# Gates' chain moved to ScalarE, idle TensorE products at three places, and one evacuation moved at the end of layer 1

## The chip, the cores and the metric

One core of one Trainium2 chip runs the whole program in one launch. The metric is the device time of an execution in microseconds (us), taken as the median of several runs. All tensors are fp32. TensorE runs at one of two granted clocks, 1.2 and 2.4 GHz, which the profile shows as 0.5 and 1.0.

## The reference

Two layers over x of 64 batches, 32 rows and 512 columns. Layer 0 is cross attention to a context of 257 rows, self attention and a linear layer with LoRA. Layer 1 begins with a gate over channels, then has self attention and a linear layer. The part around the change is the gate of layer 1:

```python
mu = jnp.mean(z, axis=(0, 2), keepdims=True)
var = jnp.mean((z - mu) ** 2, axis=(0, 2), keepdims=True)
zn = (z - mu) * jax.lax.rsqrt(var + EPS)
zn = zn * gamma.reshape(1, -1, 1) + beta.reshape(1, -1, 1)
return jax.nn.sigmoid(jax.nn.relu(zn))
...
A_S1 = _norm_active(_conv1d(crucial_x, conv_w), bn_gamma, bn_beta)
A_S2 = _norm_active(_conv1d(subcrucial_x, conv_w), bn_gamma, bn_beta)
return crucial_features * A_S1 + subcrucial_features * A_S2
```

The convolution has two input channels (maximum and mean over the channels chosen, or over the rest) and 7 taps along 512 positions. Its mean and variance go over all 64 batches and 512 positions. So no tile of layer 1 can begin before every tile of layer 0 has ended and the statistics are known.

## The kernel before

x is kept in SBUF as 16 tiles of 128 rows (4 batches of 32 rows each). A first phase computes the cross attention of layer 0 (to about 1470 us of the span). The rest is `phase_rest`: `layer0` (self attention and LoRA layer, to about 1810 us), `mix_gates` (the gate's convolution, statistics and sigmoid, once for all batches) and `layer1`. Each of the three is a block of its own, with an end that all engines reach before the next block begins.

`layer0` and `layer1` work in four lanes: tile t uses lane t % 4, with PSUM banks `low` and `high` of 512 columns each. `over_lanes` writes out the order of the stages by hand: each stage has a slot number (`SLOTS0`, `SLOTS1`), each tile of the first eight and of the last four a start number (`STARTS0`, `STARTS1`), and every engine issues its stages in the order of start plus slot. The first stages are unrolled, the middle is a loop over four tiles that runs twice, and the last are unrolled again. An engine works through its queue strictly in that order. A stage waits for a semaphore against t + 1.

The stages that the change touches, with their lines:

- `tile_stats` (L926 to L935), on VectorE: bn_stats, bn_aggr and the addition of EPS, each waiting for the one before through semaphores "stats" and "aggr" of `norm_sems`.
- The end of `layer0` on TensorE: the last stage is `turn3` (four transposes, L961). On VectorE the last stage is `reduce_part` (L1344), of the two halves of the last tile.
- `mix_gates`: TensorE's convolution of 20 products of 128x128 by 128x128 (L1399) into one bank of PSUM, and two sums over partitions by a product with a matrix of ones (L1403, L1405). VectorE masks w_ffn (L1428), then copies the convolution to SBUF (L1431), sums (L1433), forms the mean (L1435), subtracts it (L1437), squares (L1441), sums (L1443), forms the variance (L1445), multiplies by the inverse root (L1447), applies gamma and beta (L1450) and relu (L1452). GpSimd takes the root (L1411, two instructions), ScalarE the sigmoid of 512 columns (L1417), VectorE writes `blend` (L1454, L1455).
- `layer1` on TensorE: `turn_mix` (L1537), `turn1` (L961), `qkv` (L1544 and L1547), `scores` (L1555), `values` (L1564), `project` (L1571), `turn2` (L961), `ffn` (L1577). On ScalarE: `xnT1` (L1591), `evac_qk` (L1598), `exps` (L1603), `spread_p` (L1611), `evac_ot` (L1617), `xnT2` (L1591). On VectorE among others `gate`, `add_rest`, `mix` (L1628, L1635, L1641), `add_mix` (L1645), `turn_probs` (L1682 to L1690), `add_proj` (L1695), `add_ffn` (L1699).

By the order numbers, TensorE's first stages in layer 1 are turn_mix of tiles 0 and 1, turn1 of tile 0, qkv of tile 0. Its last are values and project of tile 14, values of tile 15, turn2 of tile 14, project of tile 15, ffn of tile 14, turn2 and ffn of tile 15. ScalarE issues exps of tile 15 (41.722) ahead of evac_ot of tile 14 (41.749).

## Time and profile before

| | us |
|---|---|
| median of 3 runs | 2084.58 |
| the three runs | 2083.96, 2084.58, 2088.28 |
| the profiled execution's own time | 2082.45 |
| its span, first to last instruction | 2080.6 |
| mean granted clock over the span | 0.989 |

Start times in the rows are us from the start of the span. The first number of a timeline row is the start, the second the duration; "x8" counts instructions. One fp32 product on TensorE is two records, so a product of 128 columns is x2. In brackets stands how long the engine had been idle and what ended that. A row of the chain of waits has start, duration and the work.

### The profile page before, as it was taken

Reading aid. Unit: us, or ns where it says so; the run is one execution under the profiler, and the core shown is the slowest. Engines: PE = TensorE matmul, PEld = TensorE weight load, DVE = VectorE, ACT = ScalarE, POOL = GpSimd, SP = SyncE. Lnnn points to the kernel's source line nnn. Section 1 sums busy time; section 2 is a strip of 40 time slices with the busy share of each in tenths; the row PEclk is TensorE's granted clock in tenths of the full one; section 3 lists DMA queues with packets and bytes.
Section 4 is the critical chain, followed back from the end, with each engine's and each line's share of the span. In section 5 each row is a group of like instructions: output and inputs, shape, how many; then the busy total and the mean of one; then the engine's idle time right before and its main releaser. Section 6 shows DMA issues by size and latency. Waiting matters only on the chain. (4 is left out here: it accounts for less than half of the span.)

```text
span 2080.6 us, 36577 instructions
## 1 busy us (share of the span) xinstructions
PE 2011.5 (97%) x11304; PEld 1563.5 (75%) x11304; DVE 1296.1 (62%) x4403; ACT 740.4 (36%) x2037; POOL 677.5 (33%) x1068
## 2 busy tenths in 40 slices
PE   9999999999999999999999999999899999779997
PEld 7878778887887878788787878887566666455664
DVE  4745648475574836548474564847477676667775
ACT  3434434343343434334343433433232323122332
POOL 3333324233232422324242332423332333133332
PEclk9999999999999999999999999999999999889999
DMA  7100101010010101001010010111100000000000
GB/s 286 43 25 25 30 14 39 16 30 24 24 30 24 30 15 32 21 24 30 24 30 24 24 30 14 30 47 41 46 1 1 1 0 30 1 1 21 21 15 26
DMA packets 52572, 62.19 MB, mean 30 GB/s; under 512 B 14258, under 2 KB 48242, under 8 KB 51619
## 3 DMA queue, kind: packets, MB, share of 16 engines
q1 hardware_dynamic: 52514, 61.46, 9.4%
q8 instruction: 32, 0.52, 0.1%
q14 instruction: 26, 0.21, 0.0%
HBM read 54.00 MB, written 4.29 MB: 28 GB/s over the span
## 5 line engine op out<-in xcount | busy, mean ns | idle before, releaser
L438 PE MATMUL psLane<-hid,WkT 128*128 128x289 f32 x1536 | 402.4, 407 | 0.0
L438 PEld LDWEIGHTS psLane<-hid,WkT 128*128 128x128 f32 x1536 | 283.4, 190 | 72.3
L656 ACT ACTIVATE probs<-psLane,nmax 128x289 f32<-128x289 f32 x256 | 126.0, 497 | 430.1 <-DVE nmax L765 430.1
L622 ACT ACTIVATE KT<-psLane 96x289 f32<-96x289 f32 (+2 forms) x384 | 155.5, 405 | 149.9 <-PE psLane L438 147.7
L360 POOL TENSOR_TENSOR w_o<-w_o 128x192 f32<-128x192 f32 x64 | 39.0, 610 | 455.2 <-ACT w_o L631 455.2
L805 DVE MAX8 top<-work 128x8 f32<-128x257 f32 x512 | 180.3, 414 | 2.7
L320 POOL TENSOR_TENSOR tails<-probs,unit 128x66 f32<-128x66 f32 x128 | 38.2, 299 | 436.8 <-ACT probs L656 406.0
L428 PE MATMUL psLane<-xnT,WqT 128*128 128x128 f32 x1536 | 176.6, 275 | 0.0
L428 PEld LDWEIGHTS psLane<-xnT,WqT 128*128 128x128 f32 x1536 | 174.7, 192 | 0.3 <-issue 0.3
L525 PE MATMUL psLane<-WoT,OT 128*128 128x512 f32 x384 | 169.0, 597 | 1.4 <-DVE OT L785 1.4
L790 DVE TENSOR_TENSOR X<-X,psLane 128x512 f32 (+1 forms) x16 | 11.0, 688 | 253.9 <-PE psLane L525 253.9
L631 ACT ACTIVATE w_o<-psLane 128x384 f32<-128x384 f32 (+1 forms) x256 | 113.5, 451 | 153.4 <-PE psLane L451 153.4
L471 PE MATMUL psLane<-KT,QT 96*128 96x289 f32 x512 | 146.1, 406 | 1.3 <-ACT QT L645 1.3
L525 PEld LDWEIGHTS psLane<-WoT,OT 128*128 128x128 f32 x384 | 73.1, 192 | 86.7 <-issue 85.0
L762 DVE TENSOR_REDUCE rmax<-psLane 128x2 f32<-128x578 f32 x128 | 97.1, 758 | 64.2 <-PE psLane L471 62.8
L779 DVE TENSOR_TENSOR O<-psLane,rinv 128x384 f32<-128x384 f32 x64 | 35.7, 558 | 158.2 <-PE psLane L498 143.6
L940 POOL TENSOR_TENSOR lane_rstd<-lane_veps,neghalf 128x1 f32<-128x1 f32 x79 | 53.0, 671 | 188.8 <-DVE lane_veps L935 188.8
L471 PEld LDWEIGHTS psLane<-KT,QT 96*128 96x128 f32 x512 | 90.8, 190 | 22.7 <-issue 7.2
L494 PEld LDWEIGHTS psLane<-V,probsT 128*128 128x128 f32 x512 | 84.4, 190 | 30.0 <-issue 11.9
L451 PE MATMUL psLane<-WvT,hid 128*128 128x192 f32 x512 | 104.2, 326 | 0.0
L451 PE MATMUL psLane<-w_ffn 128*128 128x192 f32 x512 | 104.1, 326 | 0.0
L809 DVE MATCH_REPLACE8 work<-top,hid 128x257 f32<-128x257 f32 x256 | 102.2, 411 | 0.0
(213 smaller groups left out, 4126.7 us busy)
## 6 DMA issues: line engine op xcount, KB each, us to landing
hid<-in_ctxT SPq DMA_DIRECT2D x64, 514.0 KB, 3.8
y<-X SPq DMA_DIRECT2D x16, 256.0 KB, 2.0
X<-in_x SPq DMA_DIRECT2D x1, 3584.0 KB, 20.9
WqT<-in_WqT SPq DMA_DIRECT2D x4, 768.0 KB, 9.1
Vtail<-Vlat SPq DMA_DIRECT2D x128, 24.0 KB
WoT<-in_WoT SPq DMA_DIRECT2D x1, 3072.0 KB, 11.6
w_qkv<-in_w_qkv SPq DMA_DIRECT2D x2, 1536.0 KB, 6.3
w_ffn<-in_w_ffn SPq DMA_DIRECT2D x2, 1024.0 KB, 7.0
```

What stands on the lines that cost most here:

```text
L428: mm = pe.matmul(out[:, P * r:P * r + P], WqT[:, c, w:w + P], xnT[:, c, :], start=(c == 0), stop=(c == DC - 1))
L438: mm = pe.matmul(out[:, 0:S], WkT[:, c, P * k:P * k + P], hid[:, j, c, :], start=(c == 0), stop=(c == DC - 1))
L451: mm = pe.matmul(out, left(c), right(c), start=(c == 0), stop=(c == 1))
L471: mm = pe.matmul(psS[:, g % 2, 0:S], QT[:, g, j, :], KT[:, j % 2, g, :], start=True, stop=True)
L494: pe.matmul(out, probsT[:, g % 2, 0, :], V[:, j % 2, 0, cols], start=(g % 2 == 0), stop=False)
L525: mm = pe.matmul(psM, OT[:, n // G, n % G].rearrange("p j q -> p (j q)"), WoT[:, n, :], start=(n == 0), stop=(n == NKT * G - 1))
L622: ins = act.activation(KT[at:at + hi - lo, j % 2, g, :], psKV[lo:hi, kv_bank(t, 7 * j + k), 0:S], ACT.Copy)
L631: act.activation(vproducts[:, 2 * f:2 * f + n, :].rearrange("p a n -> p (a n)"), psKV[:, kv_bank(t, 7 * j + 3 + f), 0:VH * n], ACT.Copy).t ...
L656: act.activation(probs[:, g, :], psS[:, g % 2, 0:S], ACT.Exp, bias=nmax[:, g:g + 1], scale=XSCALE, accum_out=rsum[:, j % 2, g:g + 1]).then ...
L762: dve.tensor_reduce(rmax[:, 2 * h:2 * h + 2], psS[:, :, 0:S], AX.X, ALU.max).then_inc(rmax_done, 1)
L805: ins = dve.max(top[step // 2][:, c, :], src[:, c, :] if step == 1 else work[:, c, :])
L809: ins = dve.match_replace(work[:, c, :], picked[:, c, :], src[:, c, :] if step == 2 else work[:, c, :], GONE)
```

## The change

`mix_gates` is written anew. The convolution goes into four banks, one for each 128 output positions, and signals after each; VectorE masks w_ffn in four parts and sums each bank straight from PSUM (four instructions in the place of the copy and the sum). TensorE adds the four parts up by four products with `ones`, which now holds -1/(64*512), so that the mean comes out with its sign turned. ScalarE forms the squares with their sum (Square with an accumulator, one instruction for each of the two channels w), and after the root applies scale, offset and relu in one instruction for each w, then the sigmoid for each w, the first straight into `blend`. VectorE forms scale and offset on two columns. GpSimd takes the root of both columns in one instruction. Each ScalarE part opens with an activation on a column of scratch, Sigmoid in `mix_gates`, Exp in `layer1`.

`keep_busy` issues products of `ones` with `ones` whose output nobody reads: 10 at the end of `layer0`, 6 and 12 in `mix_gates`, 8, 10 and 4 ahead of the first turn_mix, turn1 and qkv of `layer1`, 2 ahead of project of tile 14 and 7 ahead of values of tile 15. On ScalarE, evac_ot of tile 14 gets the order number 41.65 and so goes ahead of exps of tile 15 (behind spread_p of tile 14). The two semaphores of `tile_stats` become one that counts by two.

```diff
-    dve.wait_ge(n["stats"], t + 1)
+    dve.wait_ge(n["stats"], 2 * t + 1)
     dve.memset(gate[:], 0.0)
-    dve.bn_aggr(small["mv"][:, u], small["stats"][:, u]).then_inc(n["aggr"], 1)
-    dve.wait_ge(n["aggr"], t + 1)
+    dve.bn_aggr(small["mv"][:, u], small["stats"][:, u]).then_inc(n["stats"], 1)
+    dve.wait_ge(n["stats"], 2 * t + 2)
...
+CLOSING1 = {("evac_ot", NT - 2): 41.65}
...
+            pe.wait_ge(ones_done, 1 + 2 * TB)
+            keep_busy(pe, ps[:, LANES - 1], ones, 10)
...
+def keep_busy(pe, out, ones, n):
+
+    for _ in range(n):
+        pe.matmul(out[:, 0:P], ones[:], ones[:], start=True, stop=True)
...
-            mm.then_inc(conv_done, 1)
-            pe.wait_ge(step, 2)
-            pe.matmul(sums, ones[:], part[:], start=True, stop=True).then_inc(sums_done, 1)
-            pe.wait_ge(step, 6)
-            pe.matmul(sums2, ones[:], part[:], start=True, stop=True).then_inc(sums_done, 1)
+                mm.then_inc(conv_done, 1)
+            pe.wait_ge(part_done, DC)
+            for o in range(DC):
+                mm = pe.matmul(sums, ones[:], part[:, o], start=(o == 0), stop=(o == DC - 1))
+            mm.then_inc(sums_done, 1)
+            keep_busy(pe, idle, ones, 6)
+            pe.wait_ge(squares_done, 2)
+            pe.matmul(sums2, ones[:], squares[:], start=True, stop=True).then_inc(sums_done, 1)
+            keep_busy(pe, idle, ones, 12)
...
+            pool.wait_ge(moment_ready, 1)
+            pool.tensor_tensor(rstd[:], moment[:], neghalf[:].to_broadcast([P, 2]), ALU.pow).then_inc(pow_done, 1)
...
+            act.activation(scratch[:, 0:1], neghalf[:], ACT.Sigmoid).then_inc(scratch_done, 1)
+            act.wait_ge(mean_ready, 1)
+            for w in range(2):
+                act.activation(sq[:, :, w], by_which[:, w], ACT.Square, bias=minus_mean[:, w:w + 1],
+                               accum_out=squares[:, w:w + 1]).then_inc(squares_done, 1)
+            act.wait_ge(scale_done, 1)
+            act.wait_ge(offset_step, 2)
+            for k, w in enumerate((1, 0)):
+                act.activation(Z[:, :, w], by_which[:, w], ACT.Relu, bias=offset[:, w:w + 1], scale=scale[:, w:w + 1])\
+                    .then_inc(relu_done, 1)
+                act.wait_ge(relu_done, k + 1)
+                act.activation(blend[:, :, 0] if w else Z[:, :, 0], Z[:, :, w], ACT.Sigmoid).then_inc(sig_done, 1)
...
+            for o in range(DC):
+                dve.tensor_tensor(late["w_ffn"][:, o], late["w_ffn"][:, o], late["ffn_mask"][:, o], ALU.mult)
+                dve.wait_ge(conv_done, o + 1)
+                dve.tensor_reduce(part[:, o], conv[:, o].rearrange("p (w b) -> p w b", w=2),
+                                  AX.X, ALU.add).then_inc(part_done, 1)
             dve.wait_ge(sums_done, 1)
+            dve.tensor_scalar(minus_mean[:], sums, 1.0, None, ALU.mult).then_inc(mean_ready, 1)
             dve.wait_ge(sums_done, 2)
+            dve.tensor_scalar(moment[:], sums2, -1.0, EPS, ALU.mult, ALU.add).then_inc(moment_ready, 1)
             dve.wait_ge(pow_done, 1)
+            dve.tensor_scalar(scale[:], rstd[:], affine[:, 0:1], None, ALU.mult).then_inc(scale_done, 1)
+            dve.wait_ge(scale_done, 1)
+            dve.tensor_tensor(offset[:], minus_mean[:], scale[:], ALU.mult).then_inc(offset_step, 1)
+            dve.wait_ge(offset_step, 1)
+            dve.tensor_scalar(offset[:], offset[:], affine[:, 1:2], None, ALU.add).then_inc(offset_step, 1)
+            dve.wait_ge(sig_done, 2)
+            dve.tensor_tensor(blend[:, :, 1, :], Z[:, :, 0, :], blend[:, :, 0, :], ALU.subtract)
...
+            def busy_until_first(t, n):
+
+                if isinstance(t, int) and t == 0:
+                    keep_busy(pe, high(LANES - 1), ones, n)
...
+            def busy_at_end(t, n):
+
+                if isinstance(t, int) and t >= NT - 2:
+                    keep_busy(pe, high(0), ones, n[t - NT + 2])
...
+            act.activation(scratch[:], neghalf[:], ACT.Exp).then_inc(s["table_loaded"], 1)
```

## Rows read from the trace of the kernel before

**Rows 1.** Page, busy time of each engine over the span
```profile
PE 2011.5 (97%) x11304; PEld 1563.5 (75%) x11304; DVE 1296.1 (62%) x4403; ACT 740.4 (36%) x2037; POOL 677.5 (33%) x1068
```

**Rows 2.** Stretches of 5 us: PE, PEld, DVE, ACT, POOL busy, clock, DMA share, GB/s
```profile
1800.00:1805.00 5.00, 1.00 (x6) 0.71 (x4) 4.44 (x10) 0.60 (x1) 2.16 (x2) 0.68 0.00 0
...
1810.00:1815.00 5.00, 4.42 (x20) 4.42 (x21) 2.69 (x3) 1.28 (x1) 0.00 (x0) 0.50 0.01 3
1815.00:1820.00 5.00, 2.98 (x24) 2.71 (x22) 1.81 (x4) 0.00 (x0) 0.00 (x0) 0.96 0.00 0
1820.00:1825.00 5.00, 0.38 (x2) 0.30 (x2) 3.21 (x7) 0.00 (x0) 1.07 (x2) 0.72 0.00 0
```

**Rows 3.** Timeline, end of layer 0 and the convolution
```profile
1804.14 1.11 PE L961 MATMUL psLane<-ident,lane_xn 128*128 128x128 f32 x4 [4.00 <-DVE lane_xn L945]
...
1807.09 2.62 DVE L1344 TENSOR_REDUCE Y<-lanes 128x16 f32<-128x512 f32 x4
...
1810.59 7.02 PE L1399 MATMUL psLane<-Y,band 128*128 128x128 f32 x40 [5.33 <-DVE Y L1425]
```

**Rows 4.** Timeline, the gates' chain
```profile
1819.11 0.38 PE L1403 MATMUL psLane<-part,ones 128*128 128x2 f32 x2 [1.50 <-DVE part L1433]
1819.53 0.16 DVE L1435 TENSOR_SCALAR moment<-psLane 128x2 f32<-128x2 f32 x1 [0.48 <-PE psLane L1403]
...
1822.57 1.07 POOL L1411 TENSOR_TENSOR mix_rstd<-moment,neghalf 128x1 f32<-128x1 f32 x2 [14.18 <-DVE moment L1445]
...
1826.32 0.42 DVE L1455 TENSOR_TENSOR blend<-Z 128x256 f32<-128x256 f32 x1
```

**Rows 5.** Chain of waits: 16 products of 128 columns at clock 1.00
```profile
1891.00 3.57 PE psLane L1544 x32
```

**Rows 6.** Timeline, ScalarE: activation with accumulator, and groups by shape
```profile
701.68 0.49 ACT L656 ACTIVATE probs<-psLane,nmax 128x289 f32<-128x289 f32 x1
702.06 0.20 ACT L656 ACTIVATION_READ_ACCUMULATOR probs<-psLane,nmax 128x1 f32 x1
```

**Rows 7.** Groups of instructions on ScalarE, shapes apart; last number before the bar: mean ns
```profile
L1598 ACT ACTIVATE lane_QK<-psLane,b_qk 128x128 f32<-128x128 f32 x64 | 18.0, 363 | 16.6 <-PE psLane L1547 16.6
L1603 ACT ACTIVATE lane_p<-lane_p 128x256 f32<-128x256 f32 x16 | 6.7, 418 | 23.6 <-POOL lane_p L1523 23.6
L1617 ACT ACTIVATE lane_xnT<-psLane 128x256 f32<-128x256 f32 x16 | 6.1, 382 | 28.2 <-PE psLane L1564 28.2
```

**Rows 8.** Timeline, opening of layer 1 on TensorE and ScalarE
```profile
1831.77 1.11 PE L1537 MATMUL psLane<-ident,lanes 128*128 128x128 f32 x4 [1.41 <-DVE lanes L1641]
...
1834.00 1.11 PE L961 MATMUL psLane<-ident,lane_xn 128*128 128x128 f32 x4 [1.12 <-DVE lane_xn L945]
...
1835.15 0.60 ACT L1591 ACTIVATE lane_xnT<-psLane 128x512 f32<-128x512 f32 x1 [9.07 <-PE psLane L961]
...
1835.80 5.50 PE L1544 MATMUL psLane<-lane_xnT,w_qkv 128*128 128x128 f32 x32 [0.69 <-ACT lane_xnT L1591]
```

**Rows 9.** Timeline, ScalarE's table load for Exp
```profile
1851.83 1.28 ACT L1603 ACT_TABLE_LOAD   x1
```

**Rows 10.** Timeline, TensorE after transposes in layer 1
```profile
1880.19 3.54 PE L1571 MATMUL psLane<-w_o,lane_xnT 128*128 128x512 f32 x4
```

**Rows 11.** Timeline, end of layer 1
```profile
2059.93 0.64 PE L1564 MATMUL psLane<-lanes,lane_V 128*32 128x128 f32 x16 [1.11 <-ACT lanes L1611]
...
2061.29 0.37 ACT L1617 ACTIVATE lane_xnT<-psLane 128x256 f32<-128x256 f32 x1
...
2061.70 1.98 PE L1571 MATMUL psLane<-w_o,lane_xnT 128*128 128x512 f32 x4 [1.13 <-ACT lane_xnT L1617]
...
2063.73 0.69 DVE L1695 TENSOR_TENSOR X<-X,psLane 128x512 f32<-128x512 f32 x1 [0.72 <-PE psLane L1571]
...
2064.80 0.64 PE L1564 MATMUL psLane<-lanes,lane_V 128*32 128x128 f32 x16 [1.11 <-ACT lanes L1611]
```

**Rows 12.** Register instructions of VectorE's sequencer at L931; ns min/median/max
```profile
L931 DVEq ALU_OP  x8: 40/40/47, 1603.7 to 1748.6; - x8
```

96 lines of the change are left out of this document (40 added, 56 removed).

## The prediction

> **What bounds the kernel now.** I read the page first. TensorE is busy 97% of the span [rows 1], so time can be won only where TensorE waits or runs slowly, and the granted clock of 0.989 says that slow stretches are short. Views by stretch then show where they are. Between layer 0 and layer 1 TensorE is busy 1.00 us of five, then 4.42 and 2.98 for the convolution, then 0.38 of five. The clock falls in the first of these stretches (0.68), is at 1.2 GHz through 1810 to 1815, is back at 2.4 GHz for most of the next (0.96) and falls again in the last (0.72) [rows 2]. Before each fall TensorE had done almost nothing for some us; before the rise it had worked without a pause from 1810.59 [rows 3].
>
> The timeline of that stretch shows one chain. VectorE's last reduction ends at 1807.09 + 2.62 = 1809.71, the convolution runs from 1810.59 to 1817.61 [rows 3], and then VectorE, TensorE, GpSimd and ScalarE hand one small result on to the next until blend is written at 1826.32 + 0.42 = 1826.74 [rows 4]. That is 9.13 us from the end of the convolution to blend, in which no tile can move. Then layer 1 opens, still at the low clock: four transposes take 1.11 us and the first 16 products of qkv 5.50 [rows 8], where the same work at the full clock takes 3.57 [rows 5]. The end of the kernel is a second chain: project of tile 14 waits for an evacuation on ScalarE [rows 11].
>
> **The change, part by part.** The sum is made against the profiled execution, whose own time is 2082.45 (span 2080.6). It lies 2.13 us under the median of the three runs, 2084.58. One idle product is two records. At the full clock 32 records take 3.57, so one product is 0.223; at the low clock 20 records took 4.42 in the stretch from 1810 [rows 2, 5], so one is 0.44.
>
> **(a) Ten products at the end of layer 0: 0.0.** TensorE's last transposes end at 1805.25 [rows 3]. Ten products take 2.2 at the full clock and 4.4 at the low one, to 1809.65 at the latest. VectorE's reduction, ending at 1809.71, hides them; without that cover they would cost up to 4.4. The semaphore for `ones` was raised early in the layer.
>
> **(b) The convolution: -2.3.** At 2.4 GHz throughout its 40 records take 40/32 x 3.57 = 4.46, in the place of 7.02 [rows 3, 5]: -2.56. If the ten products leave the clock where it was, the gain is 0; the low bound on a worse case is all 20 products at 0.44, which is 8.8, +1.8. Before, the clock rose 4.8 us into this work (0.96 over 1815 to 1820 leaves 0.4 us at the low clock [rows 2]); now TensorE begins that work 5.3 us earlier, with a pause of about 1 us. I take almost the whole gain, because the rise before came within the convolution itself, and leave 0.26 for a late rise. VectorE's four masks of 128x512 and four small reductions fit beside it; only the last reduction stays behind.
>
> **(c) The gates' chain: -1.9.** From the end of the convolution, in us:
> - last reduction of 128 columns, no such row; between the 0.16 of a two-column VectorE instruction and the 0.42 of one of 256 [rows 4]: 0.3, with the mask ahead of it some 0.1 late, so 0.4.
> - four products for the sum in the place of one: the one took 0.38, six more records at 3.57/32 = 0.11 make it 1.05 [rows 4, 5], done at 1.5.
> - mean with its sign turned: 0.2 with its wait [rows 4], at 1.7.
> - two squares with accumulators. The nearest pair, 289 columns, starts 0.38 apart within one instruction and its reading of the accumulator, which takes 0.20 more [rows 6]. That is about 0.5 each, 1.0 for the pair of 256: 2.8. Six idle products end at 1.5 + 1.34 = 2.9, 0.1 after; this overrun is a wait that was not there.
> - second sum 0.4, variance 0.2: at 3.5.
> - GpSimd: two roots took 1.07 [rows 4], one instruction for both takes 0.55 to 0.6: 4.1.
> - scale and offset: three VectorE instructions at 0.16 [rows 4] with waits: 4.7.
> - relu, sigmoid, relu, sigmoid, each of 256 columns. A copy of 256 takes 0.38 and an exponential of 256 0.42; a bias operand makes 128 columns take 0.36, and two operands were never used together [rows 7]. I take 0.6 for a relu and 0.42 for a sigmoid: 2.05 with waits, at 6.75. Bounds: 1.6 with no cost for operands, 2.6 if each instruction waits for the last to drain.
> - the final difference, 0.42 [rows 4]: 7.2.
>
> 9.13 - 7.2 = 1.9; the bounds of its terms give 1.0 to 2.5. The 12 products behind the second sum run from 3.3 to 6.0, beside the chain. At the low clock they would reach 8.6 and hold the end of the block by 1.4. Masking w_ffn in parts, and the load of ScalarE's table in front of the scratch sigmoid, lie beside the convolution as before.
>
> **(d) The opening of layer 1: -0.5, between -1.6 and +1.6.** In the clock times of before: turn_mix of tile 1 is ready at 1831.77 by VectorE, and ends at 1832.4 with transposes of 0.60. Eight products ahead of turn_mix of tile 0 take 1.8, hidden, since VectorE needs 2.2 for its three instructions. The ten products then run to 1834.6, while turn1 was ready at 1834.00 [rows 8]: 0.6 late, which the faster transposes about make up (1835.2 against 1835.11). The four products run to 1836.1 against 1835.80, 0.3 late. Then qkv takes 3.57 rather than 5.50 [rows 5, 8]: -1.9 + 0.3 = -1.6. The other end: the clock has fallen before the ten. Between the eight and the ten products TensorE has only transposes for 3.5 us. In layer 1 there is a row for it: after waits and transposes, project took 3.54, where it takes 1.98 elsewhere [rows 10, 11]. Then the ten take 4.4 from 1832.9 to 1837.3, turn1 ends at 1838.4, four products at 1839.3 (full clock by then), and qkv starts 3.5 late but runs at full clock: +1.6. A fall with a rise halfway through the ten gives about -0.1. I take -0.5, between this and the full gain. TensorE goes from qkv straight to the next stages, so what is won there is passed on.
>
> **(e) Exp's table in front: 0.0.** The load of 1.28 [rows 9] moves to ScalarE's idle time at the start of the layer. Its reader is VectorE, which has other tiles' stages in that queue, so I take 0; at most -1.3.
>
> **(f) The end: -0.7.** values of tile 14 end at 2059.93 + 0.64 = 2060.57, and evac_ot, which waited behind exps of tile 15, ran at 2061.29. Going ahead it can start at 2060.6 and end at 2061.0, with project at 2061.02 rather than 2061.70 [rows 11]: -0.68. exps of tile 15 is queued behind it and starts at 2061.0, 0.04 late, which VectorE's sum behind it absorbs. Two products (0.45) fit before project. add_proj of tile 14 follows project directly, and so do the norm, turn2, project of 15 and both ffn, so all of it shifts. Seven products (1.56) run from 2063.0 to 2064.6; values of tile 15 start at 2064.80 as before [rows 11].
>
> **(g) One semaphore for two: +0.1.** Its value is 2t + 1 and 2t + 2, which loops have to work out in registers; such an instruction takes 0.04 [rows 12]. Outside the loops values are constants. Only layer 1's loop (16 norms) could feel it: 0 to +1.3 at two for each norm.
>
> **The sum:** -2.3 - 1.9 - 0.5 - 0.7 + 0.1 = -5.3, so 2077.2 for a profiled execution like this one. Against the median it would be 2079.3. Part of those 2.13 us may be clock falls that hit other executions at the opening and the end, where TensorE has gaps, and which idle products would fill. I take off 0.7: **2078.6**.
>
> **Rivals.** A measurement tells about 0.2%, 4.2 us, from no change; faster begins at 2080.4.
>
> *The idle products are late themselves* (0.12). The opening is at its other end: -5.3 + 0.5 + 1.6 = -3.2, which is 2081.4. For it: a row of transposes is followed by a slow product. Against it: uninterrupted work raised the clock before.
>
> *The clock before is not won back by the ten products* (0.09). The convolution stays at about 7.0 and the opening gains nothing: -1.9 - 0.7 + 0.1 = -2.5, which is 2082.1. For it: the pause of 1 us in front of the convolution. Against it: the same shape raised it before.
>
> *A table switch inside the chain* (0.08). If Square is not in the table that Sigmoid uses, the second load lands between square and sigmoid, 1.28 once or twice [rows 9] on the path: -4.0 to -2.7 against -5.3, so 2079.9 to 2081.2. In this trace copies and Identity come between Exps with no further load; Square was never used. The Trainium skill (ScalarE: Activation LUTs, "Table sets: the hidden batching unit") says that cheap functions, relu, copy, identity and abs, are in every set, and does not name Square there; its budget of 2.7 us for a switch would make this case 2081.3 to 2084.0, while the row here has 1.28.
>
> *Idle products never hold the clock* (0.05), the slower side. They multiply constants; if they do not count as work, they only stand in the queue at 0.44 each. The place is the opening: eight end 1.3 after turn_mix is ready, which shifts VectorE behind it, ten run to 11.4 us after the layer's start, turn1 ends at 12.5, four at 14.3, and qkv starts 5.5 later than the 8.8 of before. In the gates six end 2.1 later than squares do and the twelve hold the block's end 1.6 beyond before. With -0.7 at the end that is +6.4: 2091. It decides from the point where the ten products start with the clock at 1.2 GHz and end so too.
>
> **How the numbers follow.** The forecast has 0.66, with a range of its own of 2075.5 to 2081, nearly all of it faster. Faster: 0.66 and half of the table's 0.08, 0.70. Same: the late products 0.12, the clock not won 0.09, half the table's, 0.25. Slower: 0.05. The range leaves out what is slower than "not won back" and the sum of all best bounds (-2.56 - 2.5 - 1.6 - 0.7, 2077.2 in median terms, less the 2.13 if all of it was falls: 2075.1): 2075 to 2082.5.
>
> **What would show it.** Right: TensorE's clock at 1.0 in 1810 to 1822; the convolution under 5 us; from its end to the last write of blend 6.7 to 8.1; no table load between Square and Sigmoid; at the opening, first 16 products of qkv about 3.6; evac_ot of tile 14 under 0.1 us after values, project 0.45 after. Wrong: an idle product still running when turn1's xn is ready by more than 1 us; the convolution near 7; ScalarE's six instructions of the chain summing over 3.7; a wait of values of tile 15 on products ahead of it.

## The result and the profile after

The changed kernel takes 2074.75 us, the median of five executions (2074.12 to 2076.66), beside 2084.58 for the kernel before in five executions of the same session (2083.81 to 2088.28). The ratio is 0.9951, with a 95% interval of 0.9939 to 0.9962: it is faster, by 9.8 us. The forecast was 2078.6 with a range from 2075.0, so the direction was right and the time lies 0.25 us below the range. The profiled execution took 2076.66 (span 2074.5, mean clock 0.995), where the one before took 2082.45 (2080.6, 0.989). Between these two the difference is 5.8 us, against a sum of 5.3. So most of what the forecast missed lies outside its sum by parts: in what it took the medians to be beside the two profiled executions. The experiments look for that, and for the one part of the sum that came out otherwise.

The busy times of the page of after, against [rows 1]:

```profile
PE 2021.7 (97%) x11428; PEld 1575.4 (76%) x11428; DVE 1291.7 (62%) x4404; ACT 743.1 (36%) x2046; POOL 676.0 (33%) x1067
```

TensorE has 124 more records, two each for the 59 idle products and the three more of the first sum. It is 10.2 us longer busy in a span 6.1 us shorter. A busy share can't tell the two kernels apart here (97% in both): the added work gives nothing to the output and stands where TensorE would have waited.

The stretches of [rows 2] come out like this (PE, PEld, DVE, ACT, POOL busy, clock, DMA share, GB/s):

```profile
1805.00:1810.00 5.00, 4.70 (x24) 4.51 (x22) 4.89 (x9) 0.60 (x1) 1.27 (x1) 0.58 0.00 0
1810.00:1815.00 5.00, 3.89 (x34) 3.89 (x35) 3.12 (x9) 1.49 (x2) 0.00 (x0) 1.00 0.01 3
1815.00:1820.00 5.00, 4.62 (x40) 4.37 (x39) 1.51 (x6) 1.02 (x4) 0.70 (x1) 1.00 0.00 0
1820.00:1825.00 5.00, 3.32 (x30) 3.16 (x30) 2.52 (x7) 3.33 (x6) 0.00 (x0) 1.00 0.00 0
1825.00:1830.00 5.00, 2.96 (x25) 2.53 (x24) 4.23 (x11) 0.00 (x0) 0.55 (x1) 1.00 0.00 2
1830.00:1835.00 5.00, 5.00 (x47) 5.00 (x46) 4.40 (x12) 0.60 (x1) 0.93 (x1) 1.00 0.01 3
...
1875.00:1880.00 5.00, 5.00 (x12) 2.46 (x11) 2.46 (x6) 1.98 (x5) 0.00 (x0) 0.75 0.14 52
```

The clock is at its lower level while the ten products at layer 0's end run (0.58 of the stretch), and at 2.4 GHz from the first product of the convolution on, through the gates and the opening. In [rows 2] the stretches from 1810 and 1820 stand at 0.50 and 0.72. It falls once more near 1875, with project of tile 0 under it.

The timeline of after, at the end of layer 0 and through the gates, answers to [rows 3, 4]:

```profile
1804.66 1.11 PE L961 MATMUL psLane<-ident,lane_xn 128*128 128x128 f32 x4 [4.00 <-DVE lane_xn L945]
1805.57 4.13 PE L1374 MATMUL psLane<-ones 128*128 128x128 f32 x20
...
1807.61 2.63 DVE L1348 TENSOR_REDUCE Y<-lanes 128x16 f32<-128x512 f32 x4
...
1811.11 4.73 PE L1416 MATMUL psLane<-Y,band 128*128 128x128 f32 x40 [1.42 <-DVE Y L1453]
...
1815.88 0.29 DVE L1459 TENSOR_REDUCE part<-psLane 128x2 f32<-128x128 f32 x1
...
1816.23 1.05 PE L1421 MATMUL psLane<-part,ones 128*128 128x2 f32 x8 [0.39 <-DVE part L1459]
...
1817.14 1.58 PE L1374 MATMUL psLane<-ones 128*128 128x128 f32 x12
...
1817.32 0.16 DVE L1462 TENSOR_SCALAR minus_mean<-psLane 128x2 f32<-128x2 f32 x1 [1.15 <-PE psLane L1421]
1817.52 0.47 ACT L1438 ACTIVATE sq<-psLane,minus_mean 128x256 f32<-128x256 f32 x1 [5.50 <-DVE minus_mean L1462]
...
1818.59 0.38 PE L1425 MATMUL psLane<-squares,ones 128*128 128x2 f32 x2
...
1819.25 0.70 POOL L1431 TENSOR_TENSOR mix_rstd<-moment,neghalf 128x2 f32<-128x2 f32 x1 [10.32 <-DVE moment L1464]
...
1820.77 0.56 ACT L1443 ACTIVATE Z<-psLane,mix_offset,mix_scale 128x256 f32<-128x256 f32 x1 [2.23 <-DVE mix_offset L1470]
...
1821.36 0.42 ACT L1446 ACTIVATE blend<-Z 128x256 f32<-128x256 f32 x1
1821.68 0.55 ACT L1443 ACTIVATE Z<-psLane,mix_offset,mix_scale 128x256 f32<-128x256 f32 x1
...
1822.71 0.43 DVE L1472 TENSOR_TENSOR blend<-Z,blend 128x256 f32<-128x256 f32 x1 [2.04 <-ACT Z L1446]
```

The ten products end at 1809.70, 0.5 before VectorE's last reduction (1810.24), and TensorE then waits 1.42 us. The convolution takes 4.73 where it took 7.02. From its end (1815.84) to blend (1823.14) are 7.30 us where there were 9.13. No table load stands between the square and the sigmoid.

The opening of layer 1, against [rows 8]:

```profile
1825.64 0.66 PE L1561 MATMUL psLane<-ident,lanes 128*128 128x128 f32 x4 [0.18 <-DVE lanes L1678]
...
1828.17 0.66 PE L1561 MATMUL psLane<-ident,lanes 128*128 128x128 f32 x4 [1.87 <-DVE lanes L1678]
1828.66 2.40 PE L1374 MATMUL psLane<-ones 128*128 128x128 f32 x20
1829.80 0.55 DVE L945 TENSOR_SCALAR lane_xn<-X,lane_mv,lane_rstd 128x512 f32<-128x512 f32 x1 [0.66 <-POOL lane_rstd L940]
1830.89 0.60 PE L961 MATMUL psLane<-ident,lane_xn 128*128 128x128 f32 x4
1831.33 1.06 PE L1374 MATMUL psLane<-ones 128*128 128x128 f32 x8
1832.22 3.79 PE L1573 MATMUL psLane<-lane_xnT,w_qkv 128*128 128x128 f32 x32
```

The transposes take 0.66 and 0.60 where they took 1.11, and the first 16 products of qkv 3.79 where they took 5.50. xn of tile 0 is ready at 1830.35 and the ten products end at 1831.06, so they do stand in its way, by about half a microsecond: what they cost is paid, and it is less than they give.

The end of layer 1, against [rows 11]:

```profile
2054.45 0.64 PE L1599 MATMUL psLane<-lanes,lane_V 128*32 128x128 f32 x16 [1.10 <-ACT lanes L1647]
2055.02 0.71 PE L1374 MATMUL psLane<-ones 128*128 128x128 f32 x4
2055.16 0.38 ACT L1653 ACTIVATE lane_xnT<-psLane 128x256 f32<-128x256 f32 x1 [0.76 <-PE psLane L1599]
2055.59 1.99 PE L1607 MATMUL psLane<-w_o,lane_xnT 128*128 128x512 f32 x4
```

evac_ot starts 0.07 us after values of tile 14 end, where it had waited 0.72, and project starts 1.14 after values started, where that was 1.77.

**One table for all runs.** Each row is one trace, and each column is worked out from its timeline by the starts and ends of the instructions shown above: when the last turn3 of layer 0 ends; the convolution's duration; from its end to blend; from the start of layer 1's first instruction of VectorE to turn1 of tile 1 (the opening, with qkv of tile 0 in it); from there to values of tile 14 (the middle); from there to the last instruction (the tail).

| trace | last turn3 ends | convolution | chain | opening | middle | tail | last instruction ends |
|---|---|---|---|---|---|---|---|
| before | 1805.25 | 7.02 | 9.13 | 15.82 | 217.07 | 18.25 | 2078.18 |
| e1, before again | 1804.52 | 7.26 | 9.13 | 15.95 | 216.94 | 21.41 | 2080.86 |
| e5, before + end's products | 1803.70 | 7.17 | 9.13 | 15.90 | 217.00 | 18.25 | 2076.79 |
| e6, before + moved evacuation | 1807.55 | 7.41 | 9.13 | 16.02 | 216.78 | 17.62 | 2080.14 |
| e2, no idle product | 1804.43 | 7.25 | 7.30 | 16.81 | 215.67 | 19.32 | 2076.42 |
| after | 1805.77 | 4.73 | 7.30 | 14.14 | 216.87 | 17.62 | 2072.07 |
| e9, after again | 1803.18 | 4.73 | 7.29 | 14.14 | 216.97 | 17.62 | 2069.59 |
| e13, after a third time | 1805.05 | 4.73 | 7.30 | 15.78 | 215.37 | 17.62 | 2071.49 |
| e3, none at the opening | 1803.12 | 4.73 | 7.30 | 16.23 | 215.37 | 17.62 | 2070.01 |
| e4, none at the end | 1806.15 | 4.73 | 7.29 | 14.14 | 216.91 | 17.63 | 2072.49 |
| e7, none in the gates | 1805.71 | 7.04 | 7.29 | 15.13 | 216.90 | 17.63 | 2075.33 |
| e8, old chain | 1803.53 | 4.73 | 9.13 | 15.66 | 216.99 | 17.62 | 2073.31 |
| e10 | 1805.13 | 4.73 | 7.29 | 14.83 | 215.41 | 17.62 | 2070.67 |
| e11 | 1805.64 | 4.73 | 7.29 | 13.71 | 215.37 | 17.62 | 2070.45 |
| e12 | 1801.89 | 6.36 | 7.29 | 13.71 | 215.38 | 17.62 | 2068.34 |

From before to after, the difference of 6.1 us in the last instruction is +0.52 (the start of the stretch), -2.29 (convolution), -1.83 (chain), -1.68 (opening), -0.20 (middle) and -0.63 (tail). The forecast's terms for the last five were -2.3, -1.9, -0.5, +0.1 and -0.7.

The first column varies by a part of the kernel that neither change nor experiment touches before e12: the last projection of phase 1. The clock falls under it in some traces (0.66 from 1450 to 1455 in after) and not in others (1.00 in e9), here after and then e9:

```profile
1450.96 12.17 PE L525 MATMUL psLane<-WoT,OT 128*128 128x512 f32 x24 [1.45 <-DVE OT L785]
...
1449.81 10.57 PE L525 MATMUL psLane<-WoT,OT 128*128 128x512 f32 x24 [1.45 <-DVE OT L785]
```

Before, after, e4, e7, e10, e11 and e13 have it (11.95 to 12.26) and reach the end of turn3 at 1805.05 to 1806.15; e6 has more of it (13.61) and ends at 1807.55. e1, e2, e3, e5, e8 and e9 take 10.57 and end at 1803.12 to 1804.52.

### The profile page after: what moved, and what is told of

The parts are those of the page before. It is cut to its first block and busy times, and to the rows that moved or that the text cites. A ratio compares the mean times of both kernels' runs of the same rounds, so it can differ in the third digit from the quotient of the medians.

```text
span 2074.5 us, 36891 instructions
## 1 busy us (share of the span) xinstructions
PE 2021.7 (97%) x11428; PEld 1575.4 (76%) x11428; DVE 1291.7 (62%) x4404; ACT 743.1 (36%) x2046; POOL 676.0 (33%) x1067
```

## The experiments

The forecast's sum is by parts, so the first experiments remove parts, and the kernel before is run again as one of them. **My theory** after the first result: the parts are worth what the trace shows, and the rest of the 9.8 lies in clock falls which other executions of the kernel before have and the profiled one had not. **The rival:** a part is worth more than its row shows.

**e1: the kernel before, unchanged, profiled again and timed in 11 executions.**

> The kernel of before, unchanged, for the span and clock of each of its executions. Theory A (the steps of the forecast are right, and the further 4 us of the medians are stretches at the low clock that other executions of before have and the profiled one had not): the slower executions show a lower mean clock, by about 2 us of the low clock more for each us of time. Theory B (what differs from run to run is not the clock): the mean clock is the same 0.989 in executions of 2083.8 and 2088.

Measured: median 2086.37 (2083.05 to 2088.6), against 2084.32 for the 21 others of the same kernel on the same chip; the ratio of a kernel to itself is 1.0006 [0.9997, 1.0015]. The two medians differ by 2 us, and single executions by 5.5. Theory A is borne out: the spread goes with the clock. The three executions of e1 at a mean clock of 0.989 took 2083.5 in the mean, the six at 0.988 2086.4 and the two at 0.986 2088.4. From 0.989 to 0.986 is some 12 us more at 1.2 GHz for 4.9 us of time, about 2.5 for each us where 2 was expected (an estimate, since the clocks are on record with three digits). The profiled execution (2085.13) had a tail of 21.41 in the place of 18.25. These are its timeline and its stretches there, against [rows 11]:

```profile
2061.22 3.53 PE L1571 MATMUL psLane<-w_o,lane_xnT 128*128 128x512 f32 x4 [1.13 <-ACT lane_xnT L1617]
...
2068.79 3.08 PE L1571 MATMUL psLane<-w_o,lane_xnT 128*128 128x512 f32 x4
```

```profile
2060.00:2065.00 5.00, 3.87 (x20) 1.49 (x20) 2.05 (x6) 2.39 (x6) 1.67 (x2) 0.66 0.15 54
2065.00:2070.00 5.00, 2.44 (x18) 1.64 (x11) 2.04 (x7) 0.98 (x2) 0.55 (x1) 0.78 0.01 3
```

Both project of tile 14 and that of tile 15 ran at 1.2 GHz for most of their length (3.53 and 3.08, where [rows 11] have 1.98), and the granted clock is 0.66 and 0.78 in the two stretches. So the same kernel has, in some executions, two falls that cost 3.2 us together and which the profiled execution of before had not. What I had taken off for such falls was 0.7.

**e2: the changed kernel without any idle product.** Chain, moved evacuation, tables and semaphores stay.

```
-            keep_busy(pe, ps[:, LANES - 1], ones, 10)
...
-            keep_busy(pe, idle, ones, 6)
...
-            keep_busy(pe, idle, ones, 12)
...
-                    keep_busy(pe, high(LANES - 1), ones, n)
...
-                    keep_busy(pe, high(0), ones, n[t - NT + 2])
```

> The changed kernel without any idle product; chain on ScalarE and moved evacuation stay. Theory A: chain -1.9 and end -0.7 stay, convolution and opening are slow again: 2.6 under before, 2082 against 2084.6. Theory B (idle products matter little, the new chain is worth more than charged): under 2078.

Measured: 2081.8 (2077.57 to 2084.14), ratio 0.9985 [0.9976, 0.9994]. That is the 2082 of theory A. The 2.7 us against the 2084.5 of before are what the forecast has for these parts (1.9 + 0.7). Its chain is 7.30, the same as with idle products, so the forecast's overrun of six products past the squares costs nothing that can be seen. Its tail has one fall, between e1's and before's:

```profile
2063.85 3.21 PE L1602 MATMUL psLane<-w_o,lane_xnT 128*128 128x512 f32 x4
```

**e3: no idle products at the opening of layer 1 (8, 10, 4).**

```
             def busy_until_first(t, n):
-                if isinstance(t, int) and t == 0:
-                    keep_busy(pe, high(LANES - 1), ones, n)
+                return
```

> The changed kernel without the 8, 10 and 4 products of layer 1's opening. Theory A: TensorE then has only transposes from the end of the 12 products to qkv, the clock is at 1.2 GHz when qkv begins, and 1.7 us of the gain go: 2076.4. Theory B (the 12 products in the gates are enough): 2074.7, and qkv's first 16 products still take 3.8.

Measured: 2075.62 (2074.6 to 2079.35), ratio 0.9965 [0.9952, 0.9979]. That isn't slower than the changed kernel in a way that these runs can tell. Yet its trace does have the slow opening of theory A, as the first 16 products of qkv show:

```profile
1827.74 1.11 PE L961 MATMUL psLane<-ident,lane_xn 128*128 128x128 f32 x4 [1.11 <-DVE lane_xn L945]
...
1829.54 5.91 PE L1572 MATMUL psLane<-lane_xnT,w_qkv 128*128 128x128 f32 x32 [0.69 <-ACT lane_xnT L1626]
```

The opening takes 16.23, 2.09 more than in after, but the middle takes 215.37, 1.50 less: this trace has no fall near 1875. The two stretches together are 231.60 against 231.01. So in this pair of traces the 22 products save 0.6 us and not 2.1, since the fall near 1875, which after has and e3 has not, takes 1.5 back. Whether the fast opening brings that fall isn't settled: e2 and e13, slow and without it, speak for it, the kernel before, e7 and e8, with a slow opening and the fall, against it.

**e4: no idle products at the end (2, 7).**

```
             def busy_at_end(t, n):
-                if isinstance(t, int) and t >= NT - 2:
-                    keep_busy(pe, high(0), ones, n[t - NT + 2])
+                return
```

> The changed kernel without the 2 and 7 products at the end. Theory A: the end's gain is the moved evacuation; in the profiled execution nothing changes, and in executions whose clock falls between values of tile 15 and ffn of tile 14 up to 1.7 is lost: 2074.7 to 2076.2 median. Theory B (nothing falls there): 2074.7 in every run. If the seven products delay values of tile 15: 0.1 to 0.2 faster.

Measured: 2077.14 (2074.12 to 2077.8), ratio 0.9961 [0.9948, 0.9975]. Tail 17.63: in this trace the nine products are worth nothing, as (f) had them. The median is 1.0 above the changed kernel's and above what either theory allowed (at most 2076.2); the trace has no fall in its tail that would account for it.

**e5 and e6: the two parts of the end, each put alone into the kernel before.** e5 adds `keep_busy` and `busy_at_end` as above; e6 moves the evacuation:

```
+CLOSING1 = {("evac_ot", NT - 2): 41.65}
...
-    last = sorted((closing[t + LANES - NT] + x, t, n) for n, x in enumerate(slot) for t in range(NT - LANES, NT)
+    last = sorted((closing_slots.get((names[n], t), closing[t + LANES - NT] + x), t, n) for n, x in enumerate(slot) for t in range(NT - LANES, NT)
```

> The kernel of before with the 2 and 7 products at its end and nothing else. Theory A (low clock at the end is what the medians of before hold and its profile did not): from values of tile 14 to the last instruction 18.25 us, never 21.4, and the median 1 to 2 under before. Theory B (falls at the end are rare or the products fill nothing that matters): median within 0.5 of before.

> The kernel of before with evac_ot of tile 14 ahead of exps of tile 15 and nothing else. Theory A: 17.6 us from values of tile 14 to the end where the clock stays up, more where it falls; median 0.6 under before. Theory B (the moved evacuation shortens the gap so that the clock stays up as well): 1.5 or more under before.

Measured: e5 2083.53 (2080.51 to 2085.51) and e6 2084.22 (2082.02 to 2086.37), both 0.9998 [0.9989, 1.0007] of a kernel before that took 2084.15. Neither effect is resolved. Theory A of e5 wanted 1 to 2 us and that of e6 0.6; the medians moved by 0.6 and by nothing. Falls at the end are thus not what most of the spread between executions of before is made of. In the traces the tail is 18.25 in e5 and 17.62 in e6, and e6's timeline has the values and the project of tile 14 so:

```profile
2062.52 0.64 PE L1566 MATMUL psLane<-lanes,lane_V 128*32 128x128 f32 x16 [1.10 <-ACT lanes L1613]
...
2063.23 0.38 ACT L1619 ACTIVATE lane_xnT<-psLane 128x256 f32<-128x256 f32 x1 [0.76 <-PE psLane L1566]
...
2063.67 1.99 PE L1573 MATMUL psLane<-w_o,lane_xnT 128*128 128x512 f32 x4 [0.50 <-ACT lane_xnT L1619]
```

So the moved evacuation carries the whole 0.63 of (f), by the step that it named: project starts 1.15 after values. The products at the end can only be worth what they keep away. Of the five traces of the table without them (before, e1, e2, e4, e6) two have a fall in the tail; of the ten with them, none has. With so few this points one way and proves nothing.

**e7: no idle products in the gates and at layer 0's end (10, 6, 12).**

```
-            keep_busy(pe, ps[:, LANES - 1], ones, 10)
...
-            keep_busy(pe, idle, ones, 6)
...
-            keep_busy(pe, idle, ones, 12)
```

> The changed kernel without the 10, 6 and 12 products at the end of layer 0 and in the gates; those of the opening and the end stay. Theory A (they carry the clock over the whole stretch): convolution 7.0 to 7.3, low clock at the start of layer 1, the eight products take 3.5 and delay turn_mix by 1.3: 3.5 to 5 over the changed kernel, near 2079. Theory B (the opening's products restore the clock in time by themselves): only the convolution's 2.4 is lost, 2077.

Measured: 2078.68 (2078.32 to 2080.24), ratio 0.9971 [0.9961, 0.9982], as theory A had it. The convolution is back at 7.04. The opening starts with the clock at 1.2 GHz, and its first products show what a late idle product costs:

```profile
1825.67 3.75 PE L1373 MATMUL psLane<-ones 128*128 128x128 f32 x16 [4.46 <-PEq L1379]
...
1829.22 0.78 PE L1558 MATMUL psLane<-ident,lanes 128*128 128x128 f32 x4
```

Eight products take 3.75 where they took 2.02 in after, and turn_mix of tile 0 stands behind them. The clock comes back just behind them, at 1829.6, and the opening ends at 15.13, 1.0 later than in after and still 0.7 earlier than before.

**e8: the chain of before, on VectorE, inside the changed kernel**, with 8 and 16 idle products beside it for 6 and 12.

```
-            keep_busy(pe, idle, ones, 6)
+            keep_busy(pe, idle, ones, 8)
...
-            keep_busy(pe, idle, ones, 12)
+            keep_busy(pe, idle, ones, 16)
...
-            for k, w in enumerate((1, 0)):
-                act.activation(Z[:, :, w], by_which[:, w], ACT.Relu, bias=offset[:, w:w + 1], scale=scale[:, w:w + 1])\
...
+            act.wait_ge(step, 9)
+            act.activation(Z[:].rearrange("p c w b -> p (c w b)"), Z[:].rearrange("p c w b -> p (c w b)"),
+                           ACT.Sigmoid).then_inc(sig_done, 1)
```

> The changed kernel with the old chain of VectorE in the gates, idle products kept (10 before, 8 and 16 between its steps). Both theories of the clock: convolution 4.7, opening 14.1, and from the convolution's end to blend 9.1 rather than 7.3: 1.8 over the changed kernel, 2076.6. If instead the chain's cost hung on the clock (its small products at the low clock before), it is under 9.0.

Measured: 2077.85 (2076.94 to 2081.88), ratio 0.9969 [0.9957, 0.9982]. The chain is at 9.13 again with the clock at 1.00 throughout, to the hundredth what it took in [rows 2, 4], where the clock fell within it. Its length is a matter of VectorE, ScalarE, GpSimd and the hand-overs between them; TensorE's clock has no part in it. The 1.83 between 9.13 and 7.30 is (c), measured alone. The opening did not come out at the expected 14.1: it took 15.66, with the clock at 0.76 and 0.90 in the stretches from 1825 and 1830, though all of the opening's idle products are there.

**e9 and e13: the changed kernel again, twice.**

> The changed kernel, unchanged, for the spread of its executions. Theory A (clock falls that no idle product reaches, near 1450 and near 1875, still come in some executions): more executions fall in two groups, 2073.5 to 2075 and 2076 to 2078, and the median with more of them lies a little over 2074.75, up to 2076.5. Theory B (the changed kernel has no spread left): all within 2074 to 2075.

> The changed kernel once more, beside e12. Theory A: the same two groups, 2074 to 2075 and 2076.5 to 2077, and over all its executions a median between 2075 and 2076.5, so that some 1 us of the 9.8 in the first comparison was its draw of executions. Theory B (the first comparison was typical and the second was not): 2074.7 again.

Measured: 2076.71 (2074.21 to 2078.48) and 2076.12 (2074.76 to 2078.84), ratios 0.9963 [0.9949, 0.9976] and 0.9957 [0.9943, 0.997]: theory A in both, though 2078.48 and 2078.84 lie above either of its groups. Over all 15 executions the median is 2076.12, which is 1.4 above the first result and inside the forecast's range; the kernel before has 2084.49 over 68 executions (2084.58 with e1's 11), so the change is worth about 8.4 us rather than 9.8. Each against the kernel before of its own session, the three gains are 9.8, 7.7 and 9.6. Here too the spread goes with the clock: five executions at 0.996 took 2074.5 in the mean, eight at 0.995 2076.3, two at 0.993 2078.7. e13's trace has the other opening. Its timeline and its stretches:

```profile
1827.93 3.65 PE L1374 MATMUL psLane<-ones 128*128 128x128 f32 x20
1831.38 1.03 PE L961 MATMUL psLane<-ident,lane_xn 128*128 128x128 f32 x4
...
1833.13 3.80 PE L1573 MATMUL psLane<-lane_xnT,w_qkv 128*128 128x128 f32 x32
```

```profile
1830.00:1835.00 5.00, 5.00 (x37) 5.00 (x37) 4.37 (x12) 0.60 (x1) 0.92 (x1) 0.78 0.01 3
...
1875.00:1880.00 5.00, 4.97 (x17) 2.48 (x16) 3.79 (x12) 2.35 (x6) 0.74 (x1) 1.00 0.14 52
```

Here the clock fell at 1828.8, under the ten products (3.65 for 2.40), and rose at 1832.2, at the end of turn1 of tile 0 (1.03 for 0.60). Some six of the ten ran at the low clock, much as in the case that the forecast priced at "about -0.1", though it had thought of a fall ahead of them and a rise within; the opening is 15.78, -0.04. The stretch from 1875 then stands at 1.00, and the middle is 1.5 shorter.

**e10 to e12: a version that beats both?** The rows say that ten products at turn1 stand 0.5 in the way, and that a fall near 1875 is left. e10 has 7 and 3 products there for 10 and 4, and 7 ahead of turn2 of tile 1, in front of the place of that fall. e11 adds 16 ahead of the last turn3, so that the stretch at layer 0's end is filled earlier. e12 adds 25 more at the seam between phase 1 and layer 0.

```
-                busy_until_first(t, 10)
+                busy_until_first(t, 7)
...
+            def turn2(t, u):
+                if isinstance(t, int) and t == 1:
+                    keep_busy(pe, high(0), ones, 7)
+                norm_turn(pe, n5, t, u, xn, high(u), ident)
...
-                busy_until_first(t, 4)
+                busy_until_first(t, 3)
```

and, from e11 on,

```
+            def turn3(t, u):
+                if isinstance(t, int) and t == NT - 1:
+                    pe.wait_ge(ones_done, 1 + 2 * TB)
+                    keep_busy(pe, low(0), ones, 16)
+                norm_turn(pe, n3, t, u, xn, high(u), ident)
```

and, in e12 alone,

```
+                if isinstance(t, int) and (t, j) == (NT - 1, TB - 1):
+                    keep_busy(pe, psS[:, 0], ident, 3)
...
+                if isinstance(t, int) and t == NT - 1:
+                    keep_busy(pe, psS[:, 0], ident, 5)
...
+            keep_busy(pe, psS[:, 0], ident, 3)
...
+            keep_busy(pe, high(LANES - 1), ident, 14)
```

> The changed kernel with 7 and 3 products in the place of 10 and 4 at the opening, and 7 products ahead of turn2 of tile 1, where TensorE waited 1.84 and its clock then fell. Theory A: turn1 0.5 earlier, the clock no longer falls near 1875, 215.4 rather than 216.9 from turn1 of tile 1 to values of tile 14: 2 us under the changed kernel of the same call. Theory B (fewer products at the opening let the clock fall there): opening 15.5 to 16.2 rather than 14.1, gain under 0.5.

> The one before, and 16 products ahead of turn3 of tile 15, where TensorE waits 4.0 at the end of layer 0. Theory A: the clock is full there, turn3 takes 0.60 rather than 1.11 and the convolution 4.46 rather than 4.73: 0.8 less than e10. Theory B (VectorE's reduction sets the end of layer 0): only 0.3 of the convolution is won, or the products delay turn3 and cost 0.1 to 0.5.

> e11 with idle products (of the identity matrix) also where TensorE waits between the cross attention and layer 0: 3 and 5 around the last transposes of the first phase, 3 and 14 behind its last product. Theory A (the two groups of executions come from whether the clock falls near 1450, which is worth 1.5 in the last product of the phase, and layer 0 then opens at the low clock up to 1473): no fall from 1440 on in the profile, the last product takes 10.6 in every execution, no slower group, and the median is 2 to 3.5 under e11, 2072 to 2073.5. Theory B (VectorE's top-k sets the start of layer 0 and the products change nothing, or delay the first transposes): 2075 or more.

Measured: e10 2075.28 (2073.17 to 2076.0), 0.9952 [0.9938, 0.9966]; e11 2075.77 (2075.05 to 2077.5), 0.9958 [0.9944, 0.9971]; e12 2073.14 (2072.39 to 2074.63), 0.9943 [0.9929, 0.9956]. The first two can't be told from the changed kernel by their times. e10 has the short middle that its theory A wanted (215.41), but its clock fell in the opening (0.89 and 0.77 in the stretches from 1825 and 1830), and 14.83 there is neither theory's. e12 has the lowest median of all, 2.6 below e11 as its theory A had it. Its interval against the kernel before overlaps those of the changed kernel, but it was timed beside e13, on the same chip, and each of its five executions is below each of e13's (2074.63 against 2074.76). It is faster than the kernel before without doubt, and faster than the changed one in all likelihood.

e11 shows why the 16 products bring nothing where they stand, not even the 0.3 of its theory B:

```profile
1800.82 3.74 PE L1380 MATMUL psLane<-ones 128*128 128x128 f32 x32
1804.98 0.66 PE L961 MATMUL psLane<-ident,lane_xn 128*128 128x128 f32 x4 [0.43 <-DVE lane_xn L945]
...
1811.43 4.73 PE L1422 MATMUL psLane<-Y,band 128*128 128x128 f32 x40 [3.56 <-DVE Y L1459]
```

The last turn3 runs at the full clock now (0.66 for 1.11), but the convolution waits for VectorE's reduction. Its start lies 6.45 us after that turn3's start in both (1804.66 and 1811.11, 1804.98 and 1811.43). e12 shows what lies at the other seam, and a price:

```profile
1450.82 10.57 PE L529 MATMUL psLane<-WoT,OT 128*128 128x512 f32 x24 [0.39 <-DVE OT L790]
...
1807.68 6.36 PE L1428 MATMUL psLane<-Y,band 128*128 128x128 f32 x40 [3.56 <-DVE Y L1465]
```

The last projection of phase 1 takes 10.57 where e11 has 12.25, since the clock doesn't fall there (10.57 is also what the six traces above have in which it happened not to fall). Its last turn3 ends 3.75 before e11's. On the other hand the ten products at layer 0's end now run at the full clock and are done early; TensorE waits 3.56 us in place of 1.42, the clock falls (0.87 and 0.79 in the stretches from 1805 and 1810), and the convolution takes 6.36 for 4.73. Its last instruction still ends 3.7 us before that of after, and 2.1 before that of e11: the 3.75 less the 1.63 that the convolution lost. In e11 the ten products run at the full clock too and TensorE waits the same 3.56, but there the clock stays at 1.00 and the convolution takes 4.73. So ten products sized for the slow clock leave, at the fast one, a gap in which the clock may fall, and did in one of two traces.

## Why the prediction was right or wrong

**(a) Right.** The ten products ended 3.93 after the last turn3, within the 2.2 to 4.4 of the working, and VectorE's reduction hid them.

**(b) Right, with some luck in the number.** -2.29 against -2.3. The ten products won the clock back, as forecast. But the 0.26 left for a late rise was not paid for that: the clock stands at 1.00 over the whole convolution, and in e11, where it is at 1.00 ahead of it as well, the 40 records take the same 4.73. The working's 4.46, 40 records at the pace of [rows 5], was 0.27 too short because [rows 5] are from the chain of waits, which counts these 16 products of qkv only from the end of the work ahead of them. The timeline, in which 7.02 and 4.73 stand, gives the same group 3.73 in the trace of before (from 1890.84), and 3.84 where TensorE had waited ahead of it (in after from 1838.87). 3.84 and eight more records at 0.11 are the 4.73. For the same reason qkv's first 16 products take 3.79 in after and not 3.57.

**(c) Right in sum, -1.83 against -1.9.** By terms, counted from the end of the convolution: sums done 1.44 (forecast 1.5), mean 1.64 (1.7), squares 2.70 (2.8), variance 3.33 (3.5), root 4.11 (4.1), scale and offset 4.83 (4.7), activations 6.84 (6.75), blend 7.30 (7.2). The one term that was missed is GpSimd's root of two columns: 0.70 for "0.55 to 0.6". It is offset by the steps ahead of it, with the variance done 0.17 earlier. Of the bounds for a relu with two operands, the true price (0.56) is near the middle that I took.

**(d) Wrong by 1.2 in the profiled pair: the one term of the sum that was mis-sized.** "I take -0.5, between this and the full gain": the trace has -1.68, the full gain of -1.6. Within the sum, the choice between the ends is what failed. I weighed the 3.5 us of transposes between the eight and the ten products by [rows 10], a row with a fall, and after, e4 and e9 have a gap like it (in after 3.2 us, from 1825.46 to 1828.66, with transposes alone in it) without one. e13 has the fall and comes out at -0.04, near the "about -0.1" of a clock that is low for half of the ten; e8, with the same opening behind the old chain, has it too, at -0.16. So both kinds of outcome that I priced exist, three traces to two, and the mean over them would be -1.0: the mechanism was right and the size drawn too low. Nor does the opening alone decide: e3 and e13, with their slow openings, lack the fall near 1875 that costs the others 1.5, and I had no term for that. e3's medians leave the opening's products with no gain that can be measured.

**(e) Right, (g) too small to see.** No wait for a table at the first exps and none in the chain. (g) has its rows beside [rows 12], one for each of a norm's two waits:

```profile
L931 DVEq FUSED_REGOPS  x28: 46/46/53, 1604.2 to 2034.9; - x28
...
L934 DVEq ALU_OP  x28: 40/40/47, 1607.7 to 2035.7; - x28
```

The register work is there and shorter than 0.1 us for each norm. The middle of layer 1 is 0.20 shorter, not 0.1 longer, but the four traces with the old `tile_stats` differ by 0.29 among themselves there (216.78 to 217.07), so a term of 0.1 isn't resolved.

**(f) Right.** -0.63 against -0.68, by the moved evacuation alone (e6).

**"I take off 0.7" for clock falls in other executions: the step that failed.** The forecast went from its sum for a profiled execution (2077.2) to a median (2078.6) by adding the 2.13 us that the kernel before had between the two, less 0.7. It so put the changed kernel's median 1.4 above an execution like the profiled one. Measured, it is 1.9 below the profiled execution (2074.75 against 2076.66). That is 3.3 of the 3.8 us between the recorded gain of 9.8 and the forecast's 6.0; the other 0.5 is the sum (-5.8 in the profiled pair against -5.3, with -1.2 from the opening, -0.3 from the middle, +0.5 from the start of the stretch and +0.3 from outside the stretch as the largest differences). The offset of one kernel's profiled execution from its median is a draw and doesn't carry over to another kernel: after's profiled execution was the slowest of its five and has the fall near 1450 (12.17 for 10.57), in a part that the change doesn't touch; e9's, at 2074.21, has not.

What the runs show in its place: the spread of both kernels goes with the mean clock (e1, e9, e13). 1.4 of the 9.8 is the draw of five executions, since the same changed kernel has 2076.12 over 15, and by that median the forecast's 2078.6 would have been 2.5 too high and inside its range. How much of those 2.5 is the opening and how much the idle products at the end that keep falls away in other executions is argued rather than shown. For the end speak e1, with 3.2 us in its tail that [rows 11] don't have, e2, with 1.7, and the ten traces with idle products there, which show no fall; against a large share of it speaks e5, whose median moved by 0.6 only. The two profiled pairs frame it. From before to after it is -5.8; from e1 to e9, the same two kernels, -10.9 (2085.13 to 2074.21), of which the tail is 3.8 and the start of the stretch 1.3, the rest being the same parts as in the first pair to within 0.3. A gain read from one pair of traces of these kernels is uncertain by some 5 us, as much as the sum itself.

**The rivals.** The late idle products are real but small: 0.5 us at turn1, and e13 shows their other outcome in the opening while its whole time stays at 2076. "The clock is not won back by the ten products" is what e7 has by construction (7.04). It didn't happen in after, e9 or e13: the convolution took 4.73 in each. In e12 a part of it did (6.36), where the ten ran at the full clock. The table switch did not occur: Sigmoid's scratch, Square, Relu and Sigmoid run with no load between them. The Trainium skill (ScalarE: Activation LUTs, "Table sets: the hidden batching unit") says that cheap functions, relu, copy, identity and abs, are in every set, and doesn't name Square among them. In this trace Relu ran behind Sigmoid with no load, which agrees, and so did Square; whether Square is free of a load beside other functions than these no run here shows. That idle products never hold the clock is refuted by the convolution (4.73 with them, 7.04 in e7 without).

**What the parts are worth by their medians**, each against the 2076.12 of the changed kernel: the chain 1.7 (e8), the products at layer 0's end and in the gates 2.6 (e7), those at the end 1.0 (e4), those at the opening -0.5 (e3), the last two within the spread. All idle products together 5.7 (e2, whose trace also loses the opening and the tail); chain and evacuation together are the rest of the 8.4, 2.7. None of these kernels was timed beside the changed one in one session, and the kernel before differs by 1.5 between sessions (2084.15 to 2085.68). The parts taken singly add up to less than the whole, so some of what the idle products give shows only when all are gone. Which part carries that isn't settled: with a spread of 5 us between executions, runs of five don't tell 1 us.

## What to carry to other kernels

Where the clock falls while an engine waits, fill the wait with products that nobody reads, but size them from rows at the clock that they will run at, and look where their end lies against the end of the work that hides them: too few leave a gap in which it can fall again (e12, though not e11), too many, or too slow ones, stand in the way (after at turn1, e7). Profile the kernel before more than once before costing a change of a few us, since a single trace shows one draw of where the clock falls, and state the gain against a median of many executions. A chain of small hand-overs is shortened by taking steps out of it, whatever the clock of TensorE does.

## What the runs showed of the hardware that was not expected

- One program, the same inputs: the granted clock falls in other places from execution to execution. The kernel before lies between 2082.25 and 2088.71 in 24 executions of one session on one chip, and no wider over all 79 executions; where the mean clock is on record, the time goes with it (2083.5 in the mean of 33 executions at 0.989, 2086.0 of 36 at 0.988, 2088.4 of four at 0.986); and e1's profile has two falls in its tail that the first profile has not.
- A fall missed at one place may be had at another. The changed kernel has a fast opening (14.14) with a middle of 216.9 in two traces and a slow one (15.78) with a middle of 215.4 in the third. Only e11 and e12, with seven products ahead of turn2 of tile 1, have a fast opening (13.71, with three and one idle products fewer in it than after's 14.14) and a short middle (215.4) at once; e10, with the same seven, has the short middle with an opening of 14.83.
- GpSimd's root takes 0.70 us for two columns, where one instruction for each column took 1.07 for both [rows 4].
- ScalarE's relu with scale and bias both read from columns takes 0.56 for 256 columns, where a plain sigmoid takes 0.42, and the second relu starts 0.32 after the sigmoid ahead of it: two instructions that do not depend on each other overlap by 0.1.
